# Layer norms normalized on ScalarE instead of VectorE, with a new issue order on all five engines

## The reference

```python
_ln(x, g, b) = (x - mean(x)) * rsqrt(var(x) + EPS) * g + b          # over the 256 channels
# L0: 16 heads of 16
h = _ln(x);  x = x + attn_causal(h) @ W_aproj + b
x = x + attn_cross(_ln(x), context) @ Wcproj + b
x = x + gelu(_ln(x) @ W_fc + b) @ W_mproj + b                       # 1024 wide
# L1: 16 heads of 16, post-norm
x = _ln(x + attn_masked(x));  x = _ln(x + attn_cross(x, context));  x = _ln(x + relu_mlp(x))
# L2: 16 heads of 16, masked cross attention, then norm
x = _ln(attn_cross_masked(x, context) @ wo + x)
# L3: 16 heads of 64, cross attention, then norm
x = _ln(attn_cross(x, context) @ w_fc + x)
```

## Time and profile before

| | |
|---|---|
| median of 3 runs | 4522.63 us (4519.85 to 4525.02) |
| profiled execution | 4521.92 us, its span 4520.2 us |
| TensorE busy (products) | 4377.2 us, 97% |
| VectorE, ScalarE, GpSimd busy | 78%, 56%, 30% |
| mean granted TensorE clock | 0.989 of full speed |

### The profile page before, as it was taken

How to read it: one execution, slowest core, us unless ns; L and a number is a source line. 1 busy time by engine, 2 the same in 40 slices (tenths; PEclk the granted TensorE clock), 3 DMA queues, 4 the chain that set the end, 5 groups by cost and what they waited for, 6 DMA issues and landing times. The chain is left out here.

```text
span 4520.2 us, 97208 instructions
## 1 busy us (share of the span) xinstructions
PE 4377.2 (97%) x34368; PEld 3536.8 (78%) x34368; DVE 3512.6 (78%) x10917; ACT 2551.7 (56%) x6849; POOL 1376.6 (30%) x1813
## 2 busy tenths in 40 slices
PE   5999999999999899999999999979999999999998
PEld 4788888888887677777777777757888887878786
DVE  4788888888887788888888888856767676777775
ACT  3565665656555454544545445436666666666665
POOL 3334343443333133333333333322212121212121
PEclk8999999999999999999999999999999999999999
DMA  5554545444454444454544544422121212121211
GB/s 160 148 144 137 152 131 158 137 138 146 129 161 130 131 138 134 125 143 128 148 134 126 143 118 140 138 70 84 57 79 57 79 57 79 57 79 57 78 58 31
DMA packets 393271, 513.28 MB, mean 114 GB/s; under 512 B 109136, under 2 KB 360784, under 8 KB 371280
## 3 DMA queue, kind: packets, MB, share of 16 engines
q1 hardware_dynamic: 385392, 496.82, 38.0%
q10 hardware_dynamic: 7392, 10.24, 0.7%
HBM read 266.30 MB, written 236.72 MB: 111 GB/s over the span
## 5 line engine op out<-in xcount | busy, mean ns | idle before, releaser
L783 ACT ACTIVATE probs_own<-bank 128x384 f32<-128x384 f32 (+2 forms) x1280 | 598.3, 579 | 198.6 <-PE bank L1156 191.5
L1156 PE MATMUL bank<-ht,w_ff 128*128 128x256 f32 x2048 | 490.9, 383 | 0.5 <-ACT ht L681 0.5
L1156 PE MATMUL bank<-w_ff,ffh 128*128 128x256 f32 x2048 | 482.9, 381 | 0.0
L599 POOL TENSOR_SCALAR veps<-meanvar 128x2 f32<-128x2 f32 x256 | 69.3, 271 | 1220.8 <-DVE meanvar L931 1217.6
L681 ACT ACTIVATE ht<-bank,columns_l 128x256 f32<-128x256 f32 x384 | 197.0, 571 | 431.9 <-PE bank L1216 431.9
L848 ACT ACTIVATE probs_other<-bank,negmax 128x120 f32<-128x120 f32 x1024 | 354.9, 373 | 146.7 <-DVE negmax L1136 146.7
L1156 PEld LDWEIGHTS bank<-w_ff,ffh 128*128 128x128 f32 x2048 | 379.8, 190 | 47.7 <-ACT ffh L793 0.2
L1156 PEld LDWEIGHTS bank<-ht,w_ff 128*128 128x128 f32 x2048 | 373.8, 191 | 45.7 <-issue 0.8
L1017 DVE TENSOR_REDUCE nmf_other<-bank 128x4 f32<-128x480 f32 x512 | 311.5, 650 | 120.4 <-PE bank L1156 119.8
L1013 DVE CUSTOM_DVE_ANT_0 bank<-bank,mask_rows 128x256 f32<-128x256 f32 x1024 | 393.2, 472 | 6.0 <-PE bank L1156 6.0
L1156 PE MATMUL bank<-qstack_own,kstack_own 99*128 99x256 bf16 (+2 forms) x2560 | 365.5, 263 | 16.5 <-DMA qstack_own<-nm_t_own 15.3
(11 more groups left out here) (169 smaller groups left out, 10290.3 us busy)
## 6 DMA issues: line engine op xcount, KB each, us to landing
qstack_own<-q_parts SPq DMA_DIRECT2D x96, 768.0 KB, 5.9
kstack_own<-k_parts SPq DMA_DIRECT2D x64, 768.0 KB, 6.5
qstack_other<-q_parts SPq DMA_DIRECT2D x64, 768.0 KB, 6.4
q_parts<-q_parts_own SPq DMA_DIRECT2D x96, 384.0 KB, 2.6
k_parts<-k_parts_own SPq DMA_DIRECT2D x64, 384.0 KB, 2.6
q_parts<-q_parts_own SPq DMA_DIRECT2D x96, 256.0 KB, 2.8
q_parts<-other_parts SPq DMA_DIRECT2D x64, 384.0 KB, 2.5
other_words<-k_parts SPq DMA_DIRECT2D x64, 360.0 KB, 5.1
```

Source lines behind the costliest of these rows:

```text
L599: nc.gpsimd.tensor_scalar(veps[key][:, :], meanvar[key][:, :, 1], r["norms"][key]["eps"], None, ALU.add).then_inc(veps_ready.sem, 1)
L783: nc.scalar.activation(probs[key][0:rows, j % a.slots, 0:n], bank_of(u)[0:rows, 0:n], ACT.Exp, scale=a.scale).then_inc(a_done.sem, 1)
L1156: return nc.tensor.matmul(out, lhsT, rhs, start=first, stop=True, skip_group_check=True)
```

## The change

The step `norm` leaves VectorE. GpSimd's `stats` step gets two more instructions, which make `offset` = -mean * rstd, and a new ScalarE step `xhat` makes `xh` = rstd * x + offset. VectorE's next `stats` now waits for `offset` of the element before, since GpSimd reads the mean later. All lists have new orders, `START` moves by 0.03 and 0.32 periods (with the `l2` lists shifted the other way by about as much), and `SPREAD` gets entries for the first and last four elements of each pass. An unused choice (`"most"`) is added to `on_pe`.

```diff
-START = {"l0": 0.0, "l1": 32.1, "l2": 64.6}
+START = {"l0": 0.0, "l1": 32.13229, "l2": 64.92207}
 SPREAD = {
...
-    "l2": {},
+    "l2": {0: ((-0.12302, 1.01864), (0.28188, 0.84446), (0.05128, 0.99012)), 1: ((0.00092, 1.00362), (0.02516, 0.99447), (0.02696, 0.99259)), ...
...
-    xhat_ready = counts("xhat_ready", "DVE", ("norm",))
+    xhat_ready = counts("xhat_ready", "ACT", ("xhat",))
...
+    minus_ready = counts("minus_ready", "POOL", ("stats",))
+    offset_ready = counts("offset_ready", "POOL", ("stats",))
...
                 nc.gpsimd.tensor_tensor(rstd[key][:, :], veps[key][:, :], half[:, :], ALU.pow).then_inc(rstd_ready.sem, 1)
+                nc.gpsimd.tensor_scalar(offset[key][:, :], meanvar[key][:, :, 0], -1.0, None, ALU.mult).then_inc(minus_ready.sem, 1)
+                if w.new(rstd_ready, u.tag):
+                    g.wait_ge(rstd_ready.sem, w.value(rstd_ready, u.tag))
+                if w.new(minus_ready, u.tag):
+                    g.wait_ge(minus_ready.sem, w.value(minus_ready, u.tag))
+                nc.gpsimd.tensor_tensor(offset[key][:, :], offset[key][:, :], rstd[key][:, :], ALU.mult).then_inc(offset_ready.sem, 1)
...
+            elif kind == "xhat":
+                src = r["norms"][key]["src"]
+                x = x_in if src == "x_in" else xn[src]
+                if w.new(offset_ready, ("stats", key, 0)):
+                    act_e.wait_ge(offset_ready.sem, w.value(offset_ready, ("stats", key, 0)))
+                if w.new(a_full, ("norm", key, 0), 1):
+                    act_e.wait_ge(a_full.sem, w.value(a_full, ("norm", key, 0), 1))
+                if w.new(xb_half, ("xb", key, 0), 1):
+                    act_e.wait_ge(xb_half.sem, w.value(xb_half, ("xb", key, 0), 1))
+                for t in range(QT):
+                    ins = affine(xh[key][:, t, :], x[:, t, :], rstd[key][:, t:t + 1], offset[key][:, t:t + 1])
+                ins.then_inc(xhat_ready.sem, 1)
...
-                if w.new(veps_ready, u.tag, 1):
-                    dve.wait_ge(veps_ready.sem, w.value(veps_ready, u.tag, 1))
+                if w.new(offset_ready, u.tag, 1):
+                    dve.wait_ge(offset_ready.sem, w.value(offset_ready, u.tag, 1))
...
-            elif kind == "norm":
-                if w.new(moments_ready, ("stats", key, 0)):
-                    dve.wait_ge(moments_ready.sem, w.value(moments_ready, ("stats", key, 0)))
-                if w.new(rstd_ready, ("stats", key, 0)):
-                    dve.wait_ge(rstd_ready.sem, w.value(rstd_ready, ("stats", key, 0)))
...
-                for t in range(QT):
-                    ins = v.tensor_scalar(xh[key][:, t, :], x[:, t, :], meanvar[key][:, t, 0:1], rstd[key][:, t:t + 1],
-                                          ALU.subtract, ALU.mult)
-                ins.then_inc(xhat_ready.sem, 1)
```

More of the change, by code:

```diff
@@ new lines @@
+            scores_exp.own.12/1.47451 scores_exp.own.8/1.47833 probs_v.own.2/1.52445 probs_v.own.3/1.53950
+            project_v.other.0/1.60704 project_out.own.0/1.64746 project_k.other.0/1.78236 norm.1.0/1.80310
+            project_q.other.0/1.85330 scores_max.other.5/2.25353 scores_max.other.7/2.25853 scores_max.other.6/2.26353
+            scores_max.other.4/2.26853 scores_max.other.0/2.32892 scores_max.other.2/2.34156 scores_max.other.1/2.35038
+            scores_max.other.3/2.37694 negate_t.other.0/2.46418 scores_exp.other.1/2.59685 scores_exp.other.5/2.60194
@@ new lines @@
+            split_mid_q.own.0/0.68680 context.c.0/1.27576 scores_exp.own.1/1.29914 scores_exp.own.2/1.30773
+            scores_exp.own.5/1.31632 scores_exp.own.4/1.33517 scores_exp.own.3/1.34399 scores_exp.own.0/1.35258
+            scores_exp.own.7/1.36117 scores_exp.own.6/1.36976 scores_exp.own.11/1.43225 scores_exp.own.9/1.44084
+            scores_exp.own.15/1.44943 scores_exp.own.10/1.45802 scores_exp.own.13/1.47902 scores_exp.own.8/1.48840
+            scores_exp.own.12/1.49699 scores_exp.own.14/1.50558 xhat.1.0/1.77717 split_hi_k.other.0/1.80935 norm.1.0/1.82186
@@ L101 @@
[L101 to L105 removed]
+            stats.0.0/0.20954 split_rest_k.own.0/0.61019 split_rest_q.own.0/0.64087 scores_max.own.11/0.99264
@@ new lines @@
+            project_out.own.0/1.69382 stats.1.0/1.71053 project_v.other.0/1.79625 split_rest_k.other.0/1.86282
+            split_rest_q.other.0/1.92186 scores_max.other.5/2.26478 scores_max.other.6/2.27789 scores_max.other.7/2.29099
+            scores_max.other.4/2.30410 scores_max.other.0/2.34017 scores_max.other.2/2.35328 scores_max.other.3/2.38819
+            scores_max.other.1/2.40130 negate.other.0/2.42468 negate.other.1/2.42989 negate.other.2/2.43510
+            negate.other.3/2.45531 negate_t.other.0/2.47312 probs_v.other.0/2.80412 probs_v.other.1/2.81894
@@ new lines @@
+            nm_rows.own.0/1.21371 spill_q.other.0/1.92186 spill_q.other.1/1.95823 spill_q.other.2/1.99028
+            spill_k.other.2/2.00972 spill_k.other.0/2.01945 spill_k.other.1/2.02917 stack_q.other.0/2.06034
+            stack_k.other.0/2.12234 nm_rows.other.0/2.48210 store.x.0/4.26735 loads.first.0/0.03 loads.rest.0/4.00
+            loads.rest.1/4.25 loads.rest.2/4.50 loads.rest.3/4.75 loads.rest.4/5.00 loads.rest.5/5.25 loads.rest.6/5.50
+            loads.rest.7/5.75 loads.rest.8/6.00 loads.rest.9/6.25 loads.rest.10/6.50 loads.rest.11/6.75 loads.rest.12/7.00
@@ L1474, in build @@
     each(norms, "rstd", [P, QT])
+    each(norms, "offset", [P, QT])
     each(norms, "xh", [P, QT, C])
```

324 lines of the change are left out of this document (151 added, 173 removed), and 3 rows, old and new, of the table SPREAD.

## The result

The change makes the kernel slower: 4596.28 us (median of 4 runs, 4589.85 to 4598.61) against 4523.1 us, a ratio of 1.016 (95% interval 1.0148 to 1.0172). The profiled execution has a span of 4592.8 us, 72.6 more than before. The forecast was 4513 us with a range up to 4538: the sign was wrong and the range missed it.

What follows compares the result with a forecast made beforehand. TensorE, 97% busy, was taken to bound the kernel. Terms: -16 `l1` negate chain, +9 and +2 norm 1 in `l1` and `l0`, +2 `l2`, -8 seams, +2 ends: -9 from 4521.9, 4513 us; range 4484 to 4538.

Steps and rivals of the forecast that it cites:

- the seams: Between the passes, `l0` to `l1` and `l1` to `l2`: -8 us in sum, bounds +5 and -20.
- Any new wait costs its full length: Steady `l0` and `l2`: TensorE idles only 0.3 us in 400 and 1.8 us in 1300, so nothing can be gained there.
- priced at -2: Seam into `l2`: `SPREAD` moves element 0 of `l2` forward by 0.12 of a period, -2 us, between 0 and -6.
- Start and end: First element's norm 0 and last element's norm 3, nothing beside them: 0.8 us longer each, +2 us.
- The negate chain of `l1`: From `negate_t` to the scores in `l1`: both TensorE waits go, 0.5 us an element, -16 us, bounds -18 and 0.
- my sum of prices: Norm 1 in `l1`: TensorE's own work during the norm chain, summed from start-to-start distances, 6.41 us.
- the wait of 0.3 us that I forecast for `l1`: Norm 1 in `l1`: chain of 6.7 us against 6.41 us of TensorE work, in each of 31 elements, +9 us.
- The chain needs 6.7: Norm 1, start of `project_out.own` to end of `xh`: 6.7 us; against 6.65 us of work in `l0`, +2 us there.
- In `l2` norm 1 has 8.6 us: nothing there: Norm 1 in `l2`: TensorE has 8.6 us of work during the norm chain, so no wait and no cost.
- The +2 that stood for `l2`: Between `negate_t.own` and first score in `l2`: 0.2 us less work, half becomes wait, 0.07 x 31, bounds 0 and 6.
- What is queued behind `xhat` is its `ht` of the same norm: ScalarE's queue while waiting for `offset`: the `ht` behind needs `xh` anyway; in `l1` also query parts due later.
- norm chain binds: Norm 1, product as dear as the power: waits 0.8 us in `l1`, 0.55 in `l0`; +42, 4544 us; chance 0.14.

## Why the prediction was wrong

**The bound was read rightly, the seams in their direction.** "Any new wait costs its full length" in `l0` and `l2` is what happened. The seam from `l1` to `l2` gave 9.2 us and the first two distances of `l1` 8 more, against a sum of -8, so the gain was twice what was counted. All of the 9.2 is `SPREAD`'s, priced at -2, and not the lists'. The seam from `l0` gave 0.7 where -3 stood. Start and end cost 6.5, against +2.

**The negate chain of `l1`: right by itself, and half the story.** Its 13.5 us of waits fell to 1.4 in the same stretch. But the period rose by 0.5 us instead of falling by 0.5. Without offset it stays 47.5, and with the order alone it is 47.8, so this is the order: the step looked only at the place that the change repaired. Two costs stand elsewhere. The stretch of norm 1 has 7.00 us of TensorE's work where my sum of prices said 6.41. The prices were read beside other neighbours, and the new order splits `probs_other,other_words` in two. And `qstack_other<-q_parts` is a new wait of 6.9 us; what makes that DMA late wasn't followed. The 7.00 us are also why the wait of 0.3 us that I forecast for `l1` (+9 us) didn't come: the chain of 6.86 ends inside them. That it came to nothing was no merit of the forecast.

**"The chain needs 6.7" is the step that failed for `l0` and `l2`.** It was measured at one norm of `l1`, and there it came out as 6.86, with the product at 0.20 us against my 0.22. For the other passes the same number was carried over. In `l0` VectorE adds the residual 0.4 us later (2.36 us after `project_out.own` starts, not 1.94), the product takes 0.57 and the two waits of GpSimd for its own results 0.15 each: 7.65. In `l2` it is 7.89, by VectorE's multiplications, which the new order puts beside all four of GpSimd's instructions. In the kernel before only `veps` had one beside it, and during the power VectorE did nothing (in `l2` it waited 1.09 us there, for ScalarE and not for `rstd`). A sign of it stood in the trace of before, in the groups by line of `l2` (3200 to 4400 us), which I hadn't read; `veps` takes 423 ns there, against 0.22 us in `l1`:

```profile
L599 POOL TENSOR_SCALAR veps<-meanvar 128x2 f32<-128x2 f32 x53 | 22.4, 423 | 771.9 <-DVE meanvar L931 771.9
```

**"In `l2` norm 1 has 8.6 us: nothing there"** failed on its second number too. TensorE had 7.3 us of work there, as the kernel without offset shows, chiefly because my count priced 16 products of `w_other,other_parts` like others of 256 columns; they took 1.88 us. Both errors together turned "nothing" into the largest part of the loss, 37 us. The +2 that stood for `l2` was for its negate chain, where TensorE waits 0.3 us in all. In `l0` the work was 6.92 us for my 6.65, and the wait some 0.8 for my 0.05: 32 us for +2.

**"What is queued behind `xhat` is its `ht` of the same norm"** failed. ScalarE stood 331.3 us in all for `offset`, 223 times, and behind it in `l2` was the `ht` of another element.

**The rival "norm chain binds" had the effect and not the cause.** Its waits of 0.8 and 0.55 us for `l1` and `l0` came as 0 and 0.6 (0.8 by distance), and `l2`, which it left out, has 0.5 at the transpositions and 0.35 at `ht,w_own`. Its price, a product as dear as the power, is wrong: undisturbed it takes 0.20. At 0.14 its chance was far too low for a mechanism whose threshold, by my own working, was 0.15 us above the forecast.

**Why 4596.** Taking GpSimd's two instructions out gives 55 of the 73 us back; by the profiles it is 52, with 39 of them in `l2`. What stays, 21 us, is the new order's together with ScalarE's longer pair, which no run takes apart: 26 us in `l0` and 5 in `l1` between first and last, 3 at the start, against a gain of 12 in the seams and 1.5 in `l2`. In `l0` VectorE's `ff_xu` and GpSimd meet either way. With the two instructions GpSimd's product is late, without them VectorE's piece and `ctx_t_other` are: without offset the period fell by 0.1, with the MLP step moved as well by another 0.5.

## What to carry to other kernels

When an order changes, look at what the other engines do beside each short instruction of a dependent chain, and price the instruction under that load: the four of GpSimd took 1.35 us or 2.46 in `l2`, by their neighbours alone. Whichever of the two engines starts first, the other pays, so shortening one chain can make another one long. Measure a dependent chain in every stage where the change touches it, since the same chain took 5.9, 6.3 and 7.9 us in three passes of one kernel. Read TensorE's work from start to start in the order that will run, and not as a sum of prices. Where an order has been fitted to one placement of the work, moving the work and changing the order are one change: each alone cost as much as both or more.
